# Expert 0's first two steps settled by eight tiles, its first quarters moved into the attention's tail

## What is computed

```
x = x + self_attention(layernorm(x))                 # 16 heads
x = x + cross_attention(layernorm(x), ctx)           # 16 heads, ALiBi bias
s = layernorm(x) @ Wr.T + br                         # 8 experts
idx = top_k(s + biases_N, 2); val = softmax(s)[idx] / sum
a, b = split(layernorm(x) @ Wl1[n] + bl1[n])         # 512 -> 2 x 1024
y[n] = (silu(a) * b) @ Wl2[n] + bl2[n]
x = x + sum over the two chosen n of val * y[n]
```

## Time and profile before

| | us |
|---|---|
| median of 3 runs | 1713.88 (1711.39 to 1716.19) |
| profiled execution | 1710.52 |
| its span | 1708.8 |
| TensorE busy | 1646.4 (96%) |
| DVE busy | 1067.4 (62%) |
| ACT, POOL busy | 750.1, 750.5 (44% each) |

### The profile page before, as it was taken

One profiled execution on the slowest core, in us unless ns is written; L12 is line 12 of the kernel. 1 busy time (PEld: TensorE's weight loads), 2 busy tenths in 40 slices (PEclk: granted clock), 3 DMA queues, 4 the chain that ended last, 5 costly groups with the idle time before them and its releaser, 6 DMA issues. The chain is left out here.

```text
span 1708.8 us, 34515 instructions
## 1 busy us (share of the span) xinstructions
PE 1646.4 (96%) x10900; PEld 1328.8 (78%) x10900; DVE 1067.4 (62%) x1891; ACT 750.1 (44%) x1362; POOL 750.5 (44%) x845
## 2 busy tenths in 40 slices
PE   9998999999999998899999998899999999999997
PEld 8887787788787776677777776678888888888876
DVE  6564566565656556777978977754563636446653
ACT  4334344434434426566655665423352425224442
POOL 3201333332333216798888866442451514215451
PEclk9999999999999998999999999999999999999999
DMA  7667666677666749887677675337555646446774
GB/s 245 219 209 218 178 197 186 182 199 211 181 187 192 178 125 198 189 191 181 162 167 181 165 167 180 102 102 252 182 165 156 194 134 219 104 144 204 232 258 108
DMA packets 192113, 309.52 MB, mean 181 GB/s; under 512 B 22104, under 2 KB 143656, under 8 KB 184048
## 3 DMA queue, kind: packets, MB, share of 16 engines
q1 hardware_dynamic: 172480, 227.16, 48.2%
q0 software_dynamic: 14768, 46.27, 11.0%
q10 hardware_dynamic: 4752, 34.61, 5.5%
HBM read 224.30 MB, written 83.66 MB: 180 GB/s over the span
## 5 line engine op out<-in xcount | busy, mean ns | idle before, releaser
L2256 DVE TENSOR_REDUCE part_max<-a_s_bank 112x1 f32<-112x500 f32 (+1 forms) x368 | 225.1, 669 | 51.2 <-PE a_s_bank L1962 35.4
L2143 ACT ACTIVATE a_prob<-a_st_bank 125x448 f32<-125x448 f32 x384 | 189.3, 545 | 148.7 <-PE a_st_bank L1985 142.1
L2996 DVE TENSOR_TENSOR e_u_sb<-e_u_bank,e_b_row 128x512 f32<-128x512 f32 x134 | 92.3, 689 | 225.6 <-PE e_u_bank L2730 210.0
L2728 PE MATMUL e_u_bank<-e_w_hi,e_xT_hi 128*128 128x512 f32 x528 | 209.8, 397 | 1.0 <-DVE e_w_lo L2989 0.4
L2730 PE MATMUL e_u_bank<-e_w_hi,e_xT_lo 128*128 128x512 f32 x528 | 207.0, 392 | 0.0
L2729 PE MATMUL e_u_bank<-e_w_lo,e_xT_hi 128*128 128x512 f32 x528 | 206.3, 391 | 0.0
L2812 ACT ACTIVATE e_g_hi<-e_g_bank 128x256 fp32r<-128x256 f32 x133 | 51.1, 384 | 338.2 <-PE e_g_bank L2737 336.2
L2913 POOL DMA_INDIRECT out<-l_rows,e_y_row x33 | 53.0, 1605 | 286.7 <-issue 148.6
L1812 POOL TENSOR_TENSOR a_part_sum<-a_prob 125x448 f32<-125x448 f32 x128 | 146.3, 1148 | 25.1 <-ACT a_prob L2143 24.8
L1043 POOL TENSOR_TENSOR m_prob_sum<-m_prob 112x224 f32<-112x224 f32 x128 | 93.7, 736 | 137.2 <-ACT m_prob L1285 129.1
L2889 POOL TENSOR_TENSOR e_w_lo<-e_w_raw,e_w_hi 128x1024 fp32r<-128x1024 f32 x28 | 102.4, 3667 | 49.1 <-ACT e_w_hi L2822 49.1
(11 more groups left out here) (440 smaller groups left out, 4295.9 us busy)
## 6 DMA issues: line engine op xcount, KB each, us to landing
e_w_raw<-L_ffn_Wl SPq DMA_DIRECT2D x96, 512.0 KB, 10.9
e_b_row<-L_ffn_bl ACTq DMA_DIRECT2D x33, 1024.0 KB
m_c_in<-ctx POOLq DMA_DIRECT2D x12, 1000.0 KB, 6.1
v<-m_cv SPq DMA_DIRECT2D x48, 224.0 KB
a_v_sb<-v SPq DMA_DIRECT2D x32, 336.0 KB
m_q_st<-q SPq DMA_DIRECT2D x93, 112.0 KB, 3.0
m_k_st<-k SPq DMA_DIRECT2D x93, 112.0 KB, 3.0
first<-k SPq DMA_DIRECT2D x24, 375.0 KB, 5.5
```

The costliest lines, as they stand in the source:

```text
L2143: act.activation(prob[s % 2][:, hh, 2 * u:2 * u + 2, :], st_bank[n % SB][0:CR, 0:2 * S].rearrange("p (e q) -> p e q", e=2), ACT.Exp).then_ ...
L2256: dve.tensor_reduce(out, scores, AX.X, ALU.max).then_inc(s_free, 1)
L2728: pe.matmul(out, xT_hi[:, slot, k, :], w_h, start=(k == 0), stop=False)
```

## The change

Expert 0's first two steps are settled by the first go alone. `slots` now pads expert 0's count in both goes, to 256 after eight tiles and to 384 after twelve, and `choose` takes the first pad into account where it sums anew. SP loads the table's columns 0 and 1 in step 29 and column 2 at the end; POOL adds the row numbers to the first two, casts them and fetches both rows in step 30, ahead of part of its stores. TensorE turns step 0's rows right behind the last values, into a bank of the scores' ring (`turn_rows`), and computes the first two quarters (`up`) around the last `turn_h`, in place of 12 fillers; 9 fillers, not 8, stand at the end. Two PSUM banks are now kept from the attention into the experts' phase. The bias of slot 0 is loaded by SP in the attention. DVE's choice of batch 6 stands ahead of the last normalisation, and w2's first quarter is split in the attention. In `moe_phase` DVE's list begins with the first bias addition, and the step table's instructions stand behind the second and third quarters of step 0. ACT's exponential stands behind the first two gates, and its wait for `table_ready` behind step 0.

```diff
+    SETTLED = {20: 2 * STEP_ROWS, 28: FIRST_ROWS}
@@ cross_phase, SP
+                def load_spots(go, n0, n1):
+                    t0, t1 = tuple(GOES.values())[go]
+                    sp.wait_ge(entries_stored[go], 2 * (t1 - t0) * DMA)
+                    sp.sem_inc(turn, 1)
+                    sp.dma_start(table_sb[:, n0:n1, :], table...[:, n0:n1, :]).then_inc(table_loaded[go], DMA)
...
                     if batch_at(s, 1) is not None:
                         store_x2(batch_at(s, 1))
+                    if s == STORING + 4:
+                        load_spots(0, 0, 2)
...
-                sp.wait_ge(entries_stored, 2 * FIRST_TILES * DMA)
+                sp.wait_ge(last_xb_ready, 1)
+                sp.wait_ge(h_stored, (B - 1) * DMA)
+                sp.wait_ge(st_ready, st_at["h", B - 2, 1] + 1)
+                sp.wait_ge(st_free, st_at["wr",] + 1)
                 sp.sem_inc(turn, 1)
-                sp.dma_start(table_sb[:, 0:FIRST_STEPS, :], ...).then_inc(table_loaded, DMA)
+                sp.dma_start(b1_row[:, 0, :, :], b1[0:1, :]...).then_inc(b1_loaded[0], DMA)
                 store_x2(B - 1)
+                load_spots(1, 2, FIRST_STEPS)
                 store_h(B - 1)
@@ cross_phase, POOL
                 def fetch(st):
+                    pool.wait_ge(h_stored, FIRST_TILES // 2 * DMA)
+                    pool.tensor_copy(x_row[:, st:st + 1], table_sb[:, st, 0:1]).then_inc(x_row_ready, 1)
                     pool.wait_ge(x_row_ready, st + 1)
...
+                def add_own(n0, n1):
+                    pool.wait_ge(table_loaded[0], DMA)
+                    pool.tensor_tensor(table_sb[:, n0:n1, 0], ..., places["own_row"]..., ALU.add).then_inc(own_added, 1)
+                    pool.wait_ge(own_added, 1)
...
                     if s == STEPS - 2:
-                        store_entries(1, 2, 7)
-                store_entries(1, 7, 8)
+                        add_own(0, 2)
+                        for st in range(2):
+                            fetch(st)
+                        store_entries(1, 2, 4)
+                store_entries(1, 4, 6)
                 split_o(STEPS - 1)
+                store_entries(1, 6, 8)
                 pool.drain()
-                pool.wait_ge(h_stored, FIRST_TILES // 2 * DMA)
-                for st in range(2):
-                    fetch(st)
@@ cross_phase, TensorE
+                def turn_rows():
+                    pe.wait_ge(row_loaded[0], DMA)
+                    bank = s_next("rows")
+                    for kk in range(KT):
+                        last = pe.transpose(bank[:, P * kk:P * kk + P], rows[:, 0, P * kk:P * kk + P], ident[:, :])
+                    last.then_inc(s_ready, 1)
+                def up(q, k0, k1):
+                    pe.wait_ge(w1_ready, HCH + q + 1)
+                    pe.wait_ge(s_free, s_at["rows",] + 1)
+                    pe.wait_ge(of_ready, STEPS)
+                    for k in range(k0, k1):
+                        ...                                # the three matmuls of L2728 to L2730 into or_bank[q]
+                    if k1 == KT:
+                        last.then_inc(up_ready, 1)
...
+                turn_rows()
                 for t in range(2):
                     project_out(B - 1, t, 0, GROUPS - 1)
                 for t in range(2):
                     project_out(B - 1, t, GROUPS - 1, GROUPS)
-                pe.wait_ge(of_ready, STEPS)
-                keep_clock(or_bank[0], 12)
+                up(0, 0, KT)
+                up(1, 0, KT // 2)
                 turn_h(B - 1)
+                up(1, KT // 2, KT)
                 route(B - 1)
-                pe.wait_ge(row_loaded[0], DMA)
-                for kk in range(KT):
-                    last = pe.transpose(or_bank[1]..., rows[:, 0, ...], ident[:, :])
-                last.then_inc(t_ready, 1)
-                keep_clock(or_bank[0], 8)
+                pe.wait_ge(s_free, s_at["out", B - 1, 1] + 1)
+                keep_clock(s_bank[s_at["out", B - 1, 1] % SB], 9)
@@ cross_phase, ACT
                 act.wait_ge(pv_done, STEPS)
+                act.wait_ge(s_ready, s_at["rows",] + 1)
+                act.activation(xT_hi[:, 0, :, :], ..., ACT.Copy).then_inc(xhi_ready, 1)
                 for q in range(HCH):
...
                 hidden_copy(B - 1)
-                act.wait_ge(t_ready, 1)
-                act.activation(xT_hi[:, 0, :, :], or_bank[1]..., ACT.Copy).then_inc(xhi_ready, 1)
+                act.activation(one[:, :], eps[:, :], ACT.Silu)
@@ cross_phase, DVE
+                            if t0 == GOES[20][1]:
+                                then(dve.tensor_tensor(before[0:1, t0 + 1:t0 + n + 1, 0], ..., pad..., ALU.subtract))
...
-                        if t1 == FIRST_TILES:
-                            then(dve.tensor_scalar(pad, bank..., float(FIRST_ROWS), -1.0, ALU.min, ALU.mult))
-                            then(dve.scalar_tensor_tensor(before[0:1, t1, 0:1], pad, float(FIRST_ROWS), before[0:1, t1, 0:1], ALU.add, ALU.add))
+                        then(dve.tensor_scalar(pad, bank..., float(SETTLED[s]), float(SETTLED[s]), ALU.min, ALU.subtract))
+                        then(dve.tensor_tensor(before[0:1, t1, 0:1], before[0:1, t1, 0:1], pad, ALU.subtract))
...
                 normalise(STEPS - 2)
-                normalise(STEPS - 1)
                 scores_done(B - 2)
                 for part in range(5):
                     choose(B - 2, B - 1, part)
+                normalise(STEPS - 1)
+                dve.wait_ge(xhi_ready, 1)
+                dve.tensor_tensor(xT_lo[:, 0, :, :], s_bank[s_at["rows",] % SB]..., ALU.subtract).then_inc(s_free, 1)
+                dve.wait_ge(osplit_ready, STEPS)
+                split_w2(0)
                 for t in range(2):
                     residual(B - 1, t)
                 moments(B - 1)
                 hidden(B - 1)
-                dve.wait_ge(table_loaded, DMA)
-                dve.tensor_tensor(table_sb[:, 0:FIRST_STEPS, 0], ...).then_inc(rows_ready, 1)
-                dve.wait_ge(rows_ready, 1)
-                for st in range(2):
-                    dve.tensor_copy(x_row[:, st:st + 1], table_sb[:, st, 0:1]).then_inc(x_row_ready, 1)
-                for q in range(2, HCH):
-                    split_w1(q)
+                dve.wait_ge(table_loaded[1], DMA)
+                dve.tensor_tensor(table_sb[:, 2:FIRST_STEPS, 0], ..., ALU.add)
+                split_w1(2)
+                split_w1(3)
                 scores_done(B - 1)
                 for part in range(5):
                     choose(B - 1, B, part)
-                dve.wait_ge(xhi_ready, 1)
-                dve.tensor_tensor(xT_lo[:, 0, :, :], or_bank[1]..., ALU.subtract).then_inc(t_free, 1)
@@ moe_phase, SP
-                for slot in range(2):
-                    load_b1(sp, 0, slot)
-                    load_b2(sp, 0, slot)
+                load_b2(sp, 0, 0)
+                load_b1(sp, 0, 1)
+                load_b2(sp, 0, 1)
@@ moe_phase, TensorE
-                up(0, 0, 0)
-                up(0, 1, 0)
                 turn_gated(0, 0)
                 step(0, 0, 0)
                 pe.wait_ge(table_ready, 1)
@@ moe_phase, ACT
-                act.wait_ge(exp_in, 1)
-                act.activation(e[:, :, :], zs[:, :, :], ACT.Exp).then_inc(exp_out, 1)
-                act.activation(one[:, :], places["first_slot"][:, 0:1], ACT.Silu)
                 silu(0, 0)
                 gated_hi(0, 0)
                 silu(0, 1)
+                act.wait_ge(exp_in, 1)
+                act.activation(e[:, :, :], zs[:, :, :], ACT.Exp).then_inc(exp_out, 1)
+                act.activation(one[:, :], places["first_slot"][:, 0:1], ACT.Silu)
+                step(0, 0, 0)
                 act.wait_ge(table_ready, 1)
-                step(0, 0, 0)
@@ moe_phase, DVE (step_numbers is cut in two; step_experts has its last ten instructions)
+                add_bias(0, 0, 0, 1)
                 less_max()
-                split_w2(0)
-                step_numbers()
-                add_bias(0, 0, 0, 1)
-                begun_steps()
                 multiply(0, 0)
-                spots()
                 add_bias(0, 1, 0, 1)
                 gated_lo(0, 0)
                 multiply(0, 1)
                 slots()
                 split_w2(1)
-                for q in range(HCH):
-                    quarter(0, 0, 0, q, None)
-                    if q == 0:
-                        weights()
-                    if q < 2:
-                        split_w2(q + 2)
+                quarter(0, 0, 0, 0, None)
+                weights()
+                quarter(0, 0, 0, 1, None)
+                split_w2(2)
+                step_numbers()
+                quarter(0, 0, 0, 2, None)
+                split_w2(3)
+                step_experts()
+                begun_steps()
+                spots()
+                quarter(0, 0, 0, 3, None)
                 finish(0, 0, 0)
```

89 lines of the change are left out of this document (53 added, 36 removed).

## The result

The changed kernel took **1703.24 us** (median of 6 executions, 1700.68 to 1706.23) beside 1712.7 for the kernel before in the same comparison: ratio 0.9939, 95% interval 0.9921 to 0.9956. The forecast was 1710.1 with a range of 1704.3 to 1715.0, so the prediction was wrong. Three later comparisons of the two unaltered kernels gave 0.9946 (0.9926 to 0.9966), 0.9961 (0.9947 to 0.9975) and 0.9978 (0.9962 to 0.9993). Over all executions timed here the mean is 1706.4 for the changed kernel (36 of them) and 1713.6 for the one before (120), both with a standard deviation of about 3 us. (One more of the kernel before, 1827 us at a mean clock of 0.84, is left out.) The gain is therefore 7.2 us: faster, by about twice the 3.8 forecast, and by less than the first comparison said.

The account below looks back on a forecast made before the run. TensorE's pace bounds the unchanged experts' loop, so the gain is how much earlier step 2's rows turn: 5.4 less 1.6 for the clock, 3.8 us won, from the median 1713.88 to 1710.1; range 1704.3 to 1715.0.

Parts of the forecast that it names:

- POOL and the projection: Attention's end: POOL's added casts and gathers delay the split of step 30, so the projection starts 0.9 us later.
- Rival 2: Attention's end: DVE's splits hold POOL's casts, the projection starts 3.5 us late, only 1.2 us won: 1712.7; chance 0.17.
- Row 0 hidden, the first quarters in place of fillers, DVE last: Attention's end: row 0's transposes cost nothing, 18 quarter matmuls replace fillers, and DVE ends the phase at 1096.9, not TensorE.
- The experts' start: From DVE's first instruction: gated transposes at 1099.95 instead of 1108.01, TensorE at 1118.9, 1.8 us ahead of the table.
- 0.5 us wait for w2's split: Experts' start: TensorE waits about 0.5 us for the split of w2's third quarter, in place of 1.20 idle.
- rival 3: Experts' start: half clock stays from the first gated transposes, slower from 17.5 us on; 1723.5 if throughout; chance 0.11.
- The table's wait and the loop's entry: Ahead of the loop: table ready at 1120.7, entry 1.5 us, step 2's rows at 1122.2: 5.4 us won.
- Rival 1: Ahead of the loop: the table isn't the wait; step 2's rows at 1118.6, 9.0 us won: 1704.9; chance 0.30.
- The clock: Behind TensorE's new 3.3 us gap ahead of step 2's rows: a fall to half clock on the path loses 1.6 us.
- The base: Whole kernel before: gain reckoned from one profiled execution of 1710.52 us, then taken from the timed median, 1713.88.

Follow-up runs that it names:

- no fillers: The changed kernel without its nine filler matmuls behind the router and the wait ahead of them: 1708.38 us, ratio 0.9954 to the kernel before.
- the versions with the late gather: The changed kernel with step 1's gather behind the last store: 1708.5 us; with the table's addition also behind DVE's two splits: 1703.81, 1705.57 and 1705.86 us.
- early table: The changed kernel with DVE's step table instructions moved forward by one to two quarters, ahead of the slots: 1706.97 us, ratio 0.9954 to the kernel before.
- a later version: The changed kernel with step 1's gather behind the last store and the table's addition behind DVE's two splits: 1703.81, 1705.57 and 1705.86 us.

## Why the prediction was wrong, step by step

Measured from the values' end, forecast against the trace:

```
                                      forecast   after
projection starts                       2.27      2.39
attention ends (DVE)                   18.72     19.16
first instruction of the experts, DVE  20.02     20.12
first gated transposes                 21.77     21.84
TensorE done, waits for the table      40.72     41.74
step table ready                       42.52     42.82
step 2's rows turn                     44.02     44.50
```

- **POOL and the projection: right.** 0.9 us was forecast, 1.0 measured, with one of the two casts held (2.32 us). With gather 1 and the table's wait (0.47 us) moved away, the projection starts 1.9 us earlier (0.34 us behind the values' end), and 1.7 us of it reach step 2's rows: it was on the path as the forecast had it. Rival 2 fell.
- **Row 0 hidden, the first quarters in place of fillers, DVE last: right** to 0.44 us.
- **The experts' start: right.** The 1.08 us in hand ahead of the table were 1.8 in the forecast. The 0.5 us wait for w2's split did not come. A half-clock stretch of 3.4 us did, 1.7 us of lost speed, in the 18.4 us of work where rival 3 had it, and far below the 17.5 from which that rival decides:

```profile
1101.50:1105.50 4.00, 4.00 (x12) 3.14 (x12) 3.59 (x15) 3.27 (x5) 0.00 (x0) 0.58 0.99 330
```

The runs give this term its price. With 3.4 us at half clock behind the first gated transposes, the second turn of rows comes 24.2 to 24.3 us behind the ranks (six traces). With 4.3 us (no fillers) it is 24.7, and with 5.9 to 6.1 us (four traces of the versions with the late gather) 25.3 to 25.5. At 3.4 us DVE waits for no product of the third quarter, at 6 us it waits for 0.8 to 0.9 us. No trace has less than 3.4, but the price of the longer one, 1.1, is about half of 6.0 less the 1.8 us in hand that the forecast had.
- **The table's wait and the loop's entry: right.** 1.68 us at the entry (1.5 forecast; 1.5 to 1.7 in every other trace with this gap), and no change to the loop. Rival 1 fell: the table is the wait. Its 1704.9 lies nearest to the first measurement by chance, since the traces show 5.46 us won and not its 9.0. The early table shows more, that DVE's list is what comes due, wherever the table stands in it. The Trainium skill (Runtime: NRT & Kernel Launch, Instruction fetch mechanics) has a taken branch out of the fetched pages wait for a fetch, and the forecast took from it that the entry might lie nearer to its upper bound of 3.4. The entry measured half of that bound, and what it consists of no run shows.
- **The clock: the step that failed.** "A fall after the large one lies on the path ... I take 1.6." Four traces of the changed kernel have the gap (2.57 to 2.77 us) and no fall behind it. The term should have been 0, and the sum 5.4, against 5.46 measured as the mean of the stretches. That these two agree so closely is partly luck: step 2's rows came at 44.37 on average, 0.35 later than forecast, and before's stretch of 49.83 on average was 0.37 longer than the one it was reckoned from. The fall exists, with 1.3 and 3.0 us more behind the second turn of rows, in two of three traces of a later version, behind gaps of 2.51 and 2.72 us; the third had 2.60 and no fall. So the gap's length alone does not decide it, and what does was not found. On before's side the same step was blind: 3.76 us of its path were fillers at half speed, which the sum took out rightly, but the longer tails over its first quarters, 1.2 to 2.0 us, it did not know.
- **The base: also wrong.** I took one execution of before as the typical one. It had 36 us at half clock in the whole kernel, where the executions with a clock on record (114) average 52, each worked out from its mean clock and time, and a tail of 6.8 us where others have up to 13.7. The changed kernel averages 44. Within the kernel before a microsecond more at half clock goes with 0.21 us more time, within the changed one with 0.34, so 8 us less go with about 2 us: some of it is the tail, already in the 5.46. Whether that is the 1.7 us by which the mean gain (7.2, error 1.1) exceeds the stretch's 5.46, or chance, stays open. No trace shows a gain elsewhere; the profiled executions lie 5.3 us apart (1711.6 and 1706.3 on average), those of before below the mean of all.
- **The first comparison** with its 9.5 us drew the changed kernel's low end. The later medians, 1706.18 to 1707.07, lie within the forecast's range, in its lower half. With the clock's term at 0 the forecast would have been 1708.5, still 5.3 above the first measurement. The 6.9 us between forecast and measurement are the clock's 1.6, 1.2 for before's median (1713.88 became 1712.7), 2.3 by which the first comparison lies above the mean gain, and 1.8 by which that gain lies above 5.4, the part that stays open.

## What to carry to other kernels

Where an idle stretch ends in half-clock work that lies on the path, read several traces before pricing it: here its length went from 6.8 to 13.7 us between executions of the same program. Of work that is moved off such a path only what the next wait leaves is won: fillers of 3.76 us at half speed gave 1.7 us at the ranks, where TensorE then waited. Half clock on work that has time in hand costs only what exceeds that time (here 1.1 us for 6 us at half clock). A gap that is newly made need not bring a fall, so keep that term apart in the sum, with its own chance. When a queue is relieved, look at the next wait in it that does not belong there: an addition of 0.16 us, waiting for its table ahead of work that did not need it, held DVE for 3.8 us, and only with both moved was there a gain.

## What I had not expected of the hardware

- A cast of 128 numbers on POOL took 2.32 us beside a two-input subtraction of 128 x 2048 on DVE, against 0.19 alone, and ended when the subtraction did. The other way round, DVE's two TENSOR_SCALAR instructions took 1.80 each instead of 0.50 beside POOL's subtractions of 128 x 1024, so both sides can pay. Not every instruction does: DVE's statistics (BATCH_NORM_STATS2) ran beside them at their usual 1.29 us for two.
- Entering the loop cost TensorE 1.5 to 1.7 us behind its last wait, and left no gap where it did not wait.
- More fillers at the attention's end kept the clock up and gave no time back (0.9996), while moving the first eight off the path gave 2 us in the trace (0.9983).
- Half clock behind a TensorE gap of 2.5 to 2.8 us came in two of three traces of one version and in none of four of another.
